# Alignment path fetched in four parts after the weight preparation, batch-wise waits, and unused TensorE products around it, in a two-block fp32 kernel

## What is computed

```python
x = x + jnp.tanh(g_xattn[0]) * _L0_xattn_ref(ctx_1024, _layernorm(x, axis=-1))
x = x + jnp.tanh(g_ffn[0]) * _L0_ffn_ref(_layernorm(x, axis=-1), ...)
x = x + jnp.tanh(g_xattn[1]) * _L1_xattn_ref(_layernorm(x, axis=-1), ctx_1024, ctx_1024, ...)
x = x + jnp.tanh(g_ffn[1]) * _L1_ffn_ref(_layernorm(x, axis=-1), ...)
```

```python
def _align_one(small, large):
    D = _pairwise_euclidean(small, large)          # 77 x 512
    R = _dtw_cost(D)                               # cumulative cost, row by row
    i_idx, j_idx, valid = _backtrack(R, T_small, T_large)
    contrib = small[i_idx] * valid[:, None]
    return jnp.zeros((T_large, d)).at[j_idx].add(contrib)
```

## Time and profile before

| | us |
|---|---|
| three runs of the kernel, lowest, median, highest | 757.62, 759.21, 759.25 |
| the profiled execution, its own time | 759.99 |
| its span in the trace | 758.3 |
| TensorE busy, of the span | 656.2 (87%) |
| VectorE busy, of the span | 570.3 (75%) |
| ScalarE busy, of the span | 397.4 (52%) |
| GpSimd busy, of the span | 349.5 (46%) |
| mean granted clock of TensorE, of full speed | 0.903 |

### The profile page before, as it was taken

The page is one execution under the profiler, slowest core; times in us unless marked ns, Lnnn a source line. Parts: engine busy times, 40 slices in busy tenths (PEclk is TensorE's granted clock), DMA queues, the critical chain, the costliest instruction groups (busy, mean ns, idle before and its releaser), DMA issues.

```text
span 758.3 us, 13278 instructions
## 1 busy us (share of the span) xinstructions
PE 656.2 (87%) x3528; PEld 502.7 (66%) x3528; DVE 570.3 (75%) x1608; ACT 397.4 (52%) x707; POOL 349.5 (46%) x326
## 2 busy tenths in 40 slices
PE   5329523889999999999999779988989999999997
PEld 2116313667888888888888546655768888888885
DVE  6579895857777777777777784889867777777775
ACT  4624220555655655565556544544456555655654
POOL 4000130565666666666666560000356666666664
PEclk9855555699999999999999968998799999999999
DMA  6565543067776776677677100000166656665761
GB/s 155 76 86 169 166 131 62 7 147 151 161 145 139 159 154 141 146 157 154 135 154 158 28 2 2 2 2 13 38 122 153 151 133 160 156 144 138 159 153 56
DMA packets 85148, 86.50 MB, mean 114 GB/s; under 512 B 41109, under 2 KB 65294, under 8 KB 82166
## 3 DMA queue, kind: packets, MB, share of 16 engines
q1 hardware_dynamic: 77340, 79.80, 49.4%
q10 hardware_dynamic: 7769, 6.25, 3.1%
HBM read 76.84 MB, written 9.17 MB: 113 GB/s over the span
## 4 chain that ended last, share of the span: by engine, by line
PE 71%; DVE 12%; DMA 5%; issue 4%; SPq 4%; ACT 2%; POOL 2%; ACTq 1%; DVEq 0%; POOLq 0%
PE bank L1203 7%; PE bank L1204 7%; PE bank_quad L1359 7%; PE bank L1205 7%; PE bank_pair L1203 7%; PE bank_quad L1356 7%; PE bank_pair L1204 7%; PE bank_pair L1205 7%; PE bank_quad L1357 7%; DMA scr_d<-arena 3%; PE bank_pair L1252 2%; PE bank L1295 2%; DVE arena L1670 1%; PE bank_pair L1175 1%; DVE rden L1799 1%
## 5 line engine op out<-in xcount | busy, mean ns | idle before, releaser
L803 POOL TENSOR_TENSOR act_lo<-arena,act_hi 128x512 fp32r<-128x512 f32 x232 | 300.3, 1294 | 191.2 <-ACT act_hi L1003 147.7
L1017 ACT ACTIVATE arena<-bank 128x512 f32<-128x512 f32 x232 | 138.8, 598 | 183.3 <-PE bank L1205 183.3
L1903 DVE TENSOR_TENSOR bank_pair<-arena,bank_pair 128x512 f32<-128x512 f32 x220 | 152.4, 693 | 99.9 <-ACT arena L1017 70.6
L1911 DVE TENSOR_TENSOR arena<-bank_pair,arena 128x512 f32<-128x512 f32 x220 | 152.1, 691 | 17.8 <-DMA arena<-scr_mask 5.7
L1003 ACT ACTIVATE act_hi<-arena 128x512 fp32r<-128x512 f32 x232 | 144.5, 623 | 14.4 <-DVE arena L1901 7.5
L1359 PE MATMUL bank_quad<-act_lo,w_hi 128*128 128x512 f32 x232 | 93.0, 401 | 4.0 <-POOL act_lo L803 4.0
L1203 PE MATMUL bank_pair<-xn_hi,w_hi 128*128 128x512 f32 x232 | 92.8, 400 | 3.5 <-DVE arena L1911 1.8
L1203 PE MATMUL bank<-xn_hi,w_hi 128*128 128x512 f32 x232 | 93.1, 401 | 0.0
L1204 PE MATMUL bank<-xn_hi,w_lo 128*128 128x512 f32 x232 | 93.1, 401 | 0.0
L1356 PE MATMUL bank_quad<-act_hi,w_hi 128*128 128x512 f32 x232 | 93.0, 401 | 0.0
L1204 PE MATMUL bank_pair<-xn_hi,w_lo 128*128 128x512 f32 x232 | 92.1, 397 | 0.0
(11 more groups left out here) (252 smaller groups left out, 981.1 us busy)
## 6 DMA issues: line engine op xcount, KB each, us to landing
arena<-scr_mask SPq DMA_DIRECT2D x94, 512.0 KB, 6.6
scr_w<-prep_out ACTq DMA_DIRECT2D x25, 192.0 KB, 2.4
w_raw<-scr_w SPq DMA_DIRECT2D x25, 192.0 KB, 6.3
w_raw<-in_L_ffn_expert_gate_k SPq DMA_DIRECT2D x32, 64.0 KB, 5.9
w_raw<-in_L_ffn_expert_up_k SPq DMA_DIRECT2D x32, 64.0 KB, 5.6
w_raw<-in_L_ffn_expert_down_k SPq DMA_DIRECT2D x64, 32.0 KB, 5.3
prep_in<-in_L_ffn_wg SPq DMA_DIRECT2D x21, 64.0 KB, 2.0
prep_in<-in_L_ffn_wu SPq DMA_DIRECT2D x21, 64.0 KB, 2.4
```

The costliest lines, as they stand in the source:

```text
L803: nc.gpsimd.tensor_tensor(act_lo[:, k % 2, :], act_a[:, k % 2, :], act_hi[:, k % 2, :].bitcast(F32), ALU.subtract).then_inc(FF[f]["alo"], 1)
L1017: nc.scalar.activation(act_s[:, k % 2, :], ps[4 + k % 2][:], ACT.Silu).then_inc(FF[f]["silu"], 1)
L1903: nc.vector.tensor_tensor(ps[6 + i][:], act_s[:, i, :], ps[6 + i][:], ALU.mult).then_inc(FF[f]["t"], 1)
L1911: nc.vector.tensor_tensor(act_a[:, i, :], ps[6 + i][:], mask[:, j, 512 * k:512 * (k + 1)], ALU.mult).then_inc(FF[f]["act"], 1)
```

## The change

There are four edits.

1. **Where the path leaves.** `PATH_AT` is gone. SP and ScalarE run the whole preparation loop first, and all parts of the path stand behind it.
2. **Four parts.** The last piece (slots 0 to 5) becomes two, slots 2 to 5 and slots 0 to 2; GpSimd turns the first of them, VectorE the second (now 64x70 elements instead of 64x175). `ON_PARTS` has four ranges: the former last part (13 slots) becomes one of 8 slots and one of 5.
3. **Waits by batch.** The semaphores `s_path` are one for each batch instead of one for each half, and TensorE waits for batch b only before the four products of batch b.
4. **Unused products.** A helper `warm(bank, n)` issues n products of the identity (128x128, float32) with the first batch of `x` (128x512, float32) into a PSUM bank; nothing reads them, and the next real product into that bank overwrites them. 14 of them run from the moment when VectorE has done 49 of the 53 slots back, ahead of the alignment's products; 3 more stand behind the first transposes of `norm(1)`, and 2 more behind each of the next two groups of logits.

```diff
--- before.py
+++ after.py
@@ -92,8 +92,9 @@
     ROUTE1_BEFORE = {2: [(0, 0), (1, 0), (2, 1), (2, 2)], 3: [(2, 3)], 4: [(2, 4)], 5: [(2, 5)]}
     SPLIT_AT = 2
 
-    PATH_AT, PREP = 22, 4
+    PREP = 4
     MEET_PARTS, VALUE_AT = {7: range(0, 4), 8: range(4, 8), 9: range(8, 12), 10: range(12, CH)}, 16
+    WARM = (14, 3, 2)
     TURN3 = {5: 0, 7: 1}
     UP, DOWN, WIDE = P, 2 * P, 3 * P
 
@@ -263,8 +264,8 @@
 
         PIECE, AHEAD = 4, 16
         PIECES = [(SLOTS - PIECE * (g + 1), SLOTS - PIECE * g) for g in range(SLOTS // PIECE - 1)]
-        PIECES.append((0, PIECES[-1][0]))
-        ON_PARTS = [(25, SLOTS), (13, 25), (0, 13)]
+        PIECES += [(2, PIECES[-1][0]), (0, 2)]
+        ON_PARTS = [(25, SLOTS), (13, 25), (5, 13), (0, 5)]
         ON_PIECES = [1 + [p[0] for p in PIECES].index(first) for first, last in ON_PARTS]
 
         mark[0] = 0
@@ -402,7 +403,7 @@
         s_on = sem("path_cells")
         s_on_last = sem("path_last_cells")
         s_onst = [sem(f"path_stored{d}") for d in range(2)]
-        s_path = [sem(f"path_rows{d}") for d in range(2)]
+        s_path = [sem(f"path_rows{b}") for b in range(B)]
         s_xa = sem("aligned_sum")
         s_upd = sem("x_updated")
         s_out = sem("out_stored")
@@ -504,7 +505,7 @@
             at_cell = first * CW if d == 0 else (SLOTS - last) * CW - (CH - 1) * lane
             for b in range(B):
                 cells = pmask[row:row + last - first, b, PAD * (1 - d):PAD * (1 - d) + COLS].rearrange("i (c w) -> i c w", w=CW)
-                engine.dma_start(cells, at(scr_on[d, b], at_cell, [[CW, last - first], [lane, CH], [1, CW]])).then_inc(s_path[d], 16)
+                engine.dma_start(cells, at(scr_on[d, b], at_cell, [[CW, last - first], [lane, CH], [1, CW]])).then_inc(s_path[b], 16)
 
         def cells(engine, g, done):
 
@@ -594,10 +595,7 @@
             later_lanes(sp, 0)
             for g in range(PREP, GROUPS[1]):
                 load_prep(sp, g, *prep_span(g))
-                if g == PATH_AT:
-                    store_path(sp, 0, 0)
-                    load_path(sp, 0, 0)
-            for part in range(1, len(ON_PARTS)):
+            for part in range(len(ON_PARTS)):
                 store_path(sp, part, 0)
                 load_path(sp, part, 0)
             sp.wait_ge(FF[0]["wlo"], 1)
@@ -973,12 +971,9 @@
                                          scale=minus_row[:, h:h + 1]).then_inc(s_hm, 1)
                 if VALUE_AT <= g < VALUE_AT + len(CHUNK_HEADS):
                     value_block(*CHUNK_HEADS[g - VALUE_AT])
-                if g == PATH_AT:
-                    store_path(act, 0, 1)
-                    load_path(act, 0, 1)
             act.wait_ge(s_rt, 1)
             nc.scalar.activation(router[1][:], ps[6][:, 0:E1], ACT.Copy).then_inc(s_r1, 1)
-            for part in range(1, len(ON_PARTS)):
+            for part in range(len(ON_PARTS)):
                 store_path(act, part, 1)
                 load_path(act, part, 1)
 
@@ -1189,10 +1184,18 @@
             pe.wait_ge(s_khi, 1)
             pe.wait_ge(s_vb, len(CHUNK_HEADS))
             pe.wait_ge(s_r1, 1)
-            for d in range(2):
-                pe.wait_ge(s_path[d], 16 * B * len(ON_PARTS))
+
+            def warm(bank, n):
+
+                for i in range(n):
+                    nc.tensor.matmul(ps[bank][:], ident[:], x_res[:, 0:TPB, :].rearrange("p q h -> p (q h)"), start=True, stop=True)
+
+            pe.wait_ge(s_exit, SLOTS - 4)
+            pe.wait_ge(s_x[0], 16)
+            warm(0, WARM[0])
             rows = slice(0, 64 + LOWER)
             for b in range(B):
+                pe.wait_ge(s_path[b], 16 * 2 * len(ON_PARTS))
                 for q in range(TPB):
                     mm = nc.tensor.matmul(ps[4 + b][:, P * q:P * (q + 1)], pmask[rows, b, PAD + P * q:PAD + P * (q + 1)],
                                           ctx_sb[rows, b, :], start=True, stop=True)
@@ -1362,10 +1365,13 @@
                 if f == 0:
                     pe.wait_ge(s_rw[0], 16)
                     turn(1, 0)
+                    warm(4, WARM[1])
                     turn(1, 1)
                     logits(0, 0)
+                    warm(4, WARM[2])
                     turn(1, 2)
                     logits(0, 1)
+                    warm(4, WARM[2])
                     turn(1, 3)
                     logits(0, 2)
                     logits(0, B - 1)
@@ -1673,9 +1679,10 @@
                     thresholds(max(slot + 1 - AHEAD - PIECE, 0), slot + 1 - AHEAD)
                 if k % PIECE == 1 and k > PIECE:
                     entries(k // PIECE - 1)
+                if slot == 1:
+                    entries(len(PIECES) - 2)
             dve.wait_ge(s_exit, SLOTS)
-            for g in range((SLOTS - 2) // PIECE, len(PIECES)):
-                entries(g)
+            entries(len(PIECES) - 1)
             dve.wait_ge(s_ent, len(PIECES))
             cells(nc.vector, len(PIECES) - 1, s_on_last)
             first_lo(0)
```

## The result

| | before | after |
|---|---|---|
| median of 20 runs each (lowest to highest) | 759.23 us (757.62 to 762.67) | 761.98 us (760.73 to 766.15) |
| ratio of the runs, with its 95% interval | | 1.0033 (1.0021 to 1.0044) |
| span of the profiled execution | 758.3 us | 760.3 us |

By the ratio the change costs 2.5 us (0.0033 x 759.2), between 1.6 and 3.3 us; the two medians lie 2.75 us apart. The forecast was 761.5 in a range of 757.8 to 764.0.

A forecast was written before the change was run, and what follows sets the result against it. The feed-forward's start was taken to depend on when VectorE gets batch 0 (127.72) and a short TensorE part between 138 and 144 us. +2.2 for batch 0 and +0.1 at the turns gave +2.3: 761.5 in medians, range 757.8 to 764.0.

The forecast's parts named there:

- They end at ... 128.7: TensorE's 14 unused products: start 114.4, plus 12.0 at full clock and 2.3 for the slow stretch, end 128.7 (126.4 to 129.8).
- the 4.6: Time from TensorE's first unused product to the clock's rise, taken as 4.6 us from two earlier rises, 4.9 and 4.3.
- The 4.9: First of two clock rises read in the trace: TensorE begins at 12.28 and is fast at 17.16, 4.9 us.
- Batch 0, +2.2: VectorE's start on batch 0: 128.7 plus 1.23 gives 129.9 instead of 127.7, +2.2 us (-0.1 to +3.3).
- The path "by itself", -1.0 to -0.1: Path's arrival without the unused products: batch 0 at 124.5 to 125.4 against 125.5; with the wait by batch, -1.0 to -0.1 us.
- the wait by batch buys nothing once batch 0 is late: Batches behind batch 0 come every 0.86 us, VectorE takes over 2 us each, so waiting by batch gains nothing.
- The turns, "+0.1 (-0.4 to +0.4)": Unused products between the transposes and logits of `norm(1)`: small delays against a full-clock gain, +0.1 us (-0.4 to +0.4).
- The rival with a chance of 0.22: Clock falls before the three products at the turns, which run at half speed; +2.2 us more, 763.7; chance 0.22.
- I carry a shift at that point to the end one to one: From the feed-forward's start both kernels run the same instructions, so a shift there reaches the total time unchanged.
- That the clock costs nothing: Rival: clock rises as soon as the 14 products start, they end at 126.4; -0.5 us, 758.7; chance 0.18 including another reason.
- Products of 0.43 us each: Rival: each unused product takes one record's 0.43 us, 14 end at 122.7 and the path decides; -1.9, 757.3; chance 0.10.
- The fall that was left open near 136 to 139: Expected profile: TensorE's clock 1.00 from 119 on, with or without a fall near 136 to 139.

The follow-up runs named there:

- k: The kernel before with the waits by batch alone; median 759.70 us, ratio 0.9981 to the kernel before.
- e: The changed kernel without unused products and with the path in three parts instead of four; median 756.53 us, ratio 0.9961 to the kernel before.
- a: The changed kernel without any unused product (0, 0, 0); median 758.75 us, ratio 0.9993 to the kernel before.
- b: The changed kernel with only the first 14 unused products, none at the turns; median 760.51 us, ratio 1.0015 to the kernel before.
- h: The changed kernel with two more unused products between the path's products and the first turn; median 760.24 us, ratio 1.0010 to the kernel before.
- g: The changed kernel with nine unused products ahead of the path's and none at the turns; median 758.13 us, ratio 0.9975 to the kernel before.
- d: The changed kernel with ten unused products ahead of the path's and none at the turns; median 757.31 us, ratio 0.9972 to the kernel before.
- i: The changed kernel with the path in three parts, seven unused products first and none at the turns; median 756.70 us, ratio 0.9949 to the kernel before.
- j: The kernel before with the 14 unused products alone; median 762.28 us, ratio 1.0013 to the kernel before.
- c: The changed kernel with only the unused products between the turns (0, 3, 2); median 757.68 us, ratio 0.9976 to the kernel before.
- f_wait_all: The changed kernel without unused products, TensorE waiting for all four batches before the first product; median 762.73 us, ratio 1.0039 to the kernel before.

## Why the prediction was right

**All edits add up.** Counted at the update, from the single steps: waits by batch -2.21 (k against before), place behind the preparation -0.36 (e against k), the fourth part +1.82 (a against e), unused products +2.94 (the change against a). Taken in this order the sum is +2.19, which is the change against before by construction; what the steps say is that the change holds one large gain, and two losses that outweigh it.

**"They end at ... 128.7."** That is 14.6 us after the scan; the path's products began 14.72 us after it. The pair of terms held: 28 records, 12.0 us at 2.4 GHz, and a rise of the clock 4.2 us after the first product where 4.6 was taken. That the 4.6 fitted is in part luck. In seven kernels with such products ahead of the path the rise came 3.6 (b), 4.2 (after), 4.3 (h), 4.7 (g), 5.0 (d), 5.1 (i) and 5.8 us (j) after the first one: 4.6 is the middle of a spread, not a constant. And one of its two sources was misread. In the timeline of before TensorE is at work from 7.61 us on, not from 12.28, with 1.19 us idle ahead of 12.28. The granted clock reads 1.00 there from the start of the span, while the records of 512 columns take 1.06 us up to 17 us and 0.59 after it, so this rise rests on durations alone. The 4.9 hangs on where the count starts.

**Batch 0, +2.2.** Measured +2.19. From the first path product to the update it is 1.10 us; 1.23 was worked out.

**The path "by itself", -1.0 to -0.1.** a_no_products has -0.75. The landing was worked out as 10.4 to 11.3 us after the scan and was 10.79. But the sum hid its parts. That "the wait by batch buys nothing once batch 0 is late" holds where the 14 products end last; by itself it is worth 2.2 us. And the fourth part, which was costed only inside the whole, loses 1.8 of it.

**The turns, "+0.1 (-0.4 to +0.4)", is the step that failed.** +1.48 was measured, beyond both ends. The rival with a chance of 0.22 came true instead: the clock fell with the three products, 0.2 us after the first began. It gave them up to 5.2 us and a cost of 2.1 to 2.4; they took 4.44, and the cost was 1.48, because the clock was back after 3.4 us (135.1 to 138.5) and not after 4.3 to 4.9. h_filled_gap shows the cause: with the gap filled the stretch is 26.52 us, as in c (26.51), where the three products took 2.74 us as well. I weighed the rows the wrong way. Gaps of 1.17 and 1.92 us with transposes between had lost the clock before (at 136.7 by its 0.86, not 136.9), and one gap of 2.27 us followed by transposes is no weaker case. The clock fell at 135.1, behind 2.27 us of idle time and 1.00 us of transposes. The Trainium skill, "TensorE: Matmul & The Clock Gate", Part 4, has the rule that a transpose does not count as busy for the full clock. The trace agrees with it, but does not prove it. The transposes alone do not suffice: in h_filled_gap and c_turns_only the same 1.00 us of them stands behind 0.56 and 0.45 us of idle time, and the clock holds. Whether the gap alone would do it no run separates: transposes stand behind it in all of them. Either way the case deserved more than 0.22.

**Why 761.5 was near 761.98 all the same.** +2.19 and +1.48 are 3.67 us, and the runs differ by 2.5 (1.6 to 3.3). So 0.3 us or more came back later or in the scatter. "I carry a shift at that point to the end one to one" is only roughly right. Over the twelve changed kernels and the kernel before, a straight line through the time (the ratio of each) against the update has a slope of 0.90, with single kernels up to 2.2 us off it (f_wait_all). With the two measured terms on the median of before it would have been 762.9. So the number came out closer than its working by luck, from two errors of opposite sign: the missed fall of the clock, and later stretches that gave 0.9 us back in the profiled run. No run shows a mechanism for that; their scatter alone is larger.

**What the profile was to show.** The 28 records, no idle time ahead of the first product of line 1200, full clock from 119 on and a longer wait of TensorE than 1.76 us (5.32) are all there. The fall that was left open near 136 to 139 came at 135.1. The update to `act_lo` was to stay near 26.7; it is 28.13.

**The other rivals.** That the clock costs nothing fell with the windows at 0.50 up to 118.0. Products of 0.43 us each fell too: the 28 records took 14.34 us, 14 products of 0.43 would be 6.0. There the Trainium skill, "Perfetto Trace Analysis", Engine Utilization, with its half rate for low-high float32, comes to half of what a float32 product of this program takes. The 0.43 us fits one record, and a product is two.

## What to carry to other kernels

Here, work that only keeps a clock up was free as long as it ended before what the next real work waits for. Put its end (its own slow stretch included) against the landing of that data, and size it from there: at the update ten products tied, seven with three parts gained 0.8 us, and 14 lost 2.7. A wait on what is needed first and not on everything can be worth as much as all the rest: here 2.2 us at the update. Splitting a transfer that goes store, wait, load on one queue adds a round for each part; where the queue is busy when the last data is ready, the extra part makes it later.

## What the runs showed that I had not expected

- The clock's rise after the same first product, at the same place, took between 3.6 and 5.8 us in seven kernels. Where the path's own products were the first ones, it took 4.3 (before) to 6.3 us (a_no_products). What decides it stays open; the DMA traffic and the work just before differ between them, and no run separated these.
- A lost clock had a price of 1.48 us in one place and none in another: it fell at the turns in all ten kernels without products there, and the time from update to `act_lo` is 26.65 to 26.67 us in each. At the start of the feed-forward (155.6 to 162.4 in the kernel after) no cost shows above the scatter, but a fall 20 us later, in f_wait_all, goes with the longest feed-forward of all.
- One round of the path through DRAM takes 3.84 us for 420 columns and 4.07 for 280; only the 980 of the first part took more, 5.72.
- The stretch behind the first feed-forward took 320.3 to 324.1 us in kernels whose instructions there are the same, and the feed-forward itself 274.4 to 278.5. A term of 1 us can be read in a trace and not in a median.
